# Scan of a selective state-space layer: the product of delta and input is started by a ScalarE copy into PSUM

## The chip, the cores and the metric

The kernel runs on one core of a Trainium2 chip. The metric is the device time of one execution in microseconds (us); lower is better. Times in this text are us unless marked ns.

## The reference, cut to what matters

The whole program is a two-layer decoder (a state-space layer, cross attention and experts, then retention, a ternary attention block and experts again). The change touches only the first stage, for 8 sequences of 100 positions with 1024 inner channels and 16 states:

```
x = silu(conv(x_in))                       # [8, 100, 1024], the "convolved columns"
delta = softplus(x @ wd1.T @ wd2.T + b)    # [8, 100, 1024]
step: h = exp(delta * A_n) * h + (delta * x) * B_n      # for n = 0..15
      y = sum over n of h * C_n
y = (y + W_D * x) * silu(skip)
```

Every later stage needs the result of this one, so nothing else of the network runs beside it, except one by-product: while the scan runs, TensorE makes the keys of the following cross attention.

## The kernel before, in words

`mamba_scan` keeps channels on the 128 partitions and 8 x 100 = 800 columns of time. The 1024 channels are 8 tiles, numbered t = 0 to 7; each tile goes through n = 0 to 15. A Python function `turn` holds two tiles (j = 0 and 1). VectorE runs the first turn straight and the other three in a loop on the chip, so j = 0 is tile 0, 2, 4, 6.

VectorE, per tile: wait for `delta_ready`, then L698 forms `dx = delta * x` into PSUM; per n it forms `drive = dx * B_n` (L704, PSUM to PSUM) and runs the scan L707 over `decay` (SBUF) and `drive` into `state`. After the scan of n = 1 (`FINISH`) it multiplies the finished sums of the previous tile by the gate (L689, four 64x400 pieces, `finish`), which frees the two banks of sums `y`. `own` is a wait on VectorE's own counter `chain_s`, raised by one for each L698 and L704, so 17 a tile.

ScalarE, per tile: wait for `delta_ready`, then per n one exponential (L654) into a ring of RA = 3 `decay` buffers, and after it one key copied out of PSUM (L621, `take_key`, four steps behind, so at n = 0 and n = 1 it takes keys 12 and 13 of the tile before). The other work is put between them by n: the scaled x (L657, n = 6), the two gate halves (L626, n = 8 and 12), the next delta's first step (L631) and its curve Abs, Exp, Ln (L640 to L644, n = 10 to 12), the gate's Silu (L671, n = 14). Exp, Ln and Silu change tables (ACT_TABLE_LOAD).

GpSimd, per n: `seen = state * C_n` (L737), for n in `JOIN` it adds two of them (L740); it clips the next delta (L745) and at n = 13 (`ADD_AT`) adds its last part (L749), which raises `delta_ready`. TensorE makes a key per n (L762), adds `seen` into `y` with an identity (L787; at n = 0 only once `finished` says the banks are free), and makes the gate halves (L772, L775) after n = 4 and n = 8, and the next delta's product (L781). SyncE's queue stores keys and, in tile 0 only, spreads the rows B_n and C_n over all partitions (`spread_row(n + 3)`), row n + 3 once key n - 1 has been taken, which ScalarE does in its step n + 3.

`dx` is columns 0 to 799 and `drive` columns 800 to 1599 of PSUM, in banks of 512 columns.

Of the kernel before, what the change touches and what calls it, by code (L numbers as in the profile page):

```python
# [19 lines left out]
ALU = mybir.AluOpType  # L20
# [3 lines left out]
BANK = 512  # L24
NB = 8
L = 100
T = NB * L
# [61 lines left out]
class Core:  # L89
# [6 lines left out]
    def sem(self, name):  # L96
        self.counting.append(self.nc.alloc_semaphore(name))
        return self.counting[-1]
# [202 lines left out]
N_ST = 16  # L301
# [216 lines left out]
def mamba_scan(c, xc, vec, delta, proj, wd2, keys, ctx_loaded, bC, cC, spread, spread_row, negA, wk, wk_loaded, k_dram):  # L518
# [3 lines left out]
    nc, dram = c.nc, c.dram  # L522
    RA, RH, RV, RS = 3, 4, 2, 2
    with ExitStack() as ctx:
        sb = lambda s, shape, dt=F32: ctx.enter_context(nc.sbuf_tensor("ms_" + s, shape, dt))
        sem = lambda s: c.sem("ms_" + s)
        decay, state = sb("decay", [P, RA, NB, L]), sb("state", [P, RH, T])
        flat = c.psum[:, :, :].rearrange("p b n -> p (b n)")
        dx, drive = flat[:, 0:T], flat[:, T:2 * T]
        y, side_banks = [c.banks[4][:, 0:HALF], c.banks[5][:, 0:HALF]], c.banks[6:6 + RS]  # L530
        positive = sb("positive", [P, T])
        assert 2 * T <= 4 * BANK

        free = c.x_space[:, :, :].rearrange("p b d -> p (b d)")
        part = lambda at, n: free[:, D + at * T:D + (at + n) * T]
        skipw = free[:, 0:D].rearrange("p (k e) -> p k e", k=KD)
        gate, seen = part(0, 1), part(1, RV).rearrange("p (r t) -> p r t", r=RV)
        made = free[:, D + 3 * T:D + 3 * T + 2 * SH].rearrange("p (r s) -> p r s", r=2)
        cleared, decayed, chain_s = sem("cleared"), sem("decayed"), sem("vector_chain")
        skip_loaded, x_scaled = sem("skip_w_loaded"), sem("x_scaled")  # L540
        side_filled, side_taken = sem("side_filled"), sem("side_taken")
# [13 lines left out]
        tile_of = lambda t, i, j: t[:, bass.ds(i * 2 + j, 1), :].rearrange("p a t -> p (a t)")  # L555
        per, TURNS = 2 * N_ST, KE // 2

        FINISH, SCALE, SUM_X, OPEN = 1, 6, 12, 14
        GATE_AT, LAG = [4, 8], 4
        DELTA_AT, CLIP_AT, CURVE_AT, ADD_AT = [1, 2], 5, 10, 13  # L560
        JOIN = [3, 7, 9, 11]
# [54 lines left out]
        @block.scalar  # L616
        def _(act):
            def take_key(t, u, last=False):
                act.wait_ge(side_filled, at_side(t, last, "key", u) + 1)
                act.wait_ge(key_stored[u % 2], t * (8 * N_ST) + 16 * (u // 2) + 16)  # L620
                nc.scalar.copy(made[:, u % 2, :], side("key", u, last)[:, 0:SH]).then_inc(side_taken, 1)  # L621

            def take_gate(t, h, last):
                act.wait_ge(finished, t + 1)
                act.wait_ge(side_filled, at_side(t, last, "gate", h) + 1)
                nc.scalar.copy(gate[:, half(h)], side("gate", h, last)[:, 0:HALF]).then_inc(side_taken, 1)  # L626

            def take_delta(t, j, h):

                act.wait_ge(side_filled, at_side(t, False, "delta", h) + 1)  # L630
                nc.scalar.activation(delta[:, 1 - j, half(h)], side("delta", h)[:, 0:HALF], ACT.Identity,  # L631
                                     bias=vec[:, bass.ds(t + 1, 1), DC + 1:DC + 2].rearrange("p a v -> p (a v)")).then_inc(side_taken, 1)

            def curve(t, j, z):

                act.wait_ge(clipped, t + 1)
                act.wait_ge(curved, t * 3 + z + 1)
                at = delta[:, 1 - j, :]
                if z == 0:
                    ins = nc.scalar.activation(at, at, ACT.Abs)  # L640
                elif z == 1:
                    ins = nc.scalar.activation(at, at, ACT.Exp, scale=-1.0)
                else:
                    ins = nc.scalar.activation(at, at, ACT.Ln, bias=1.0)  # L644
                ins.then_inc(curved, 1)

            def tile(i, j, first=False, last=False):
                t = i * 2 + j
                if not first:
                    act.wait_ge(delta_ready, t)  # L650
                for n in range(N_ST):
                    g = j * N_ST + n
                    act.wait_ge(scanned, i * per + g + 1 + (not first and g < per % RA))
                    nc.scalar.activation(decay[:, g % RA, :, 1:], seqs(delta[:, j, :])[:, :, 1:], ACT.Exp,  # L654
                                         scale=tile_of(negA, i, j)[:, n:n + 1]).then_inc(decayed, 1)
                    if n == SCALE:
                        nc.scalar.activation(tile_of(xc, i, j), tile_of(xc, i, j), ACT.Copy,  # L657
                                             scale=tile_of(vec, i, j)[:, DC + 2:DC + 3]).then_inc(x_scaled, 1)
                    if n >= LAG:
                        take_key(t, n - LAG, last)  # L660
                    elif not first:
                        take_key(t - 1, n - LAG + N_ST)
                    if n - LAG in GATE_AT:
                        take_gate(t, GATE_AT.index(n - LAG), last)
                    if n - LAG in DELTA_AT and not last:
                        take_delta(t, j, DELTA_AT.index(n - LAG))
                    if n - CURVE_AT in range(3) and not last:
                        curve(t, j, n - CURVE_AT)
                    if n == OPEN:
                        act.wait_ge(side_taken, at_side(t, last, "gate", 1) + 1 + RS)  # L670
                        nc.scalar.activation(gate, gate, ACT.Silu).then_inc(gated, 1)  # L671

            act.wait_ge(cleared, 1)
            act.sem_inc(curved, 1)
            tile(0, 0, first=True)
            for t in range(1, KE):
                tile(t // 2, t % 2, last=t == KE - 1)
            for u in range(N_ST - LAG, N_ST):
                take_key(KE - 1, u, True)

        @block.vector
        def _(dve):
            def finish(i, j):

                dve.wait_ge(summed, (i * 2 + j) * SUMS)
                dve.wait_ge(gated, i * 2 + j)
                for r, h in quads:
                    at = placed(r, h)
                    last = nc.vector.tensor_tensor(xc[at, bass.ds(i * 2 + j - 1, 1), half(h)].rearrange("p a t -> p (a t)"),  # L689
                                                   y[r][at, :], gate[at, half(h)], ALU.mult)  # L690
                last.then_inc(finished, 1)

            def turn(i, first):
                own = Chain(dve, chain_s, i, 2 * (1 + N_ST))
                for j in range(2):
                    if not (first and j == 0):
                        dve.wait_ge(delta_ready, i * 2 + j)
                    own(nc.vector.tensor_tensor(dx, delta[:, j, :], tile_of(xc, i, j), ALU.mult))  # L698
                    for n in range(N_ST):
                        g = j * N_ST + n  # L700
                        if first and j == 0:
                            dve.wait_ge(spread[n], 32)
                        dve.wait_ge(scanned, i * per + g + RA)
                        own(nc.vector.tensor_tensor(drive, dx, bC[:, n, :], ALU.mult))  # L704
                        dve.wait_ge(decayed, i * per + g + 1)
                        dve.wait_ge(weighed, i * per + g + 1)
                        nc.vector.tensor_tensor_scan(state[:, n % RH, :],  # L707
                                                     decay[:, g % RA, :, :].rearrange("p b l -> p (b l)"),
                                                     drive, 0.0, ALU.mult, ALU.add).then_inc(scanned, 1)
                        if n == FINISH and not (first and j == 0):  # L710
                            finish(i, j)
                own.close()

            nc.vector.memset(decay[:, :, :, 0:1], 0.0).then_inc(cleared, 1)
            dve.sem_inc(scanned, RA)
            dve.sem_inc(finished, 1)
            turn(0, True)
            with dve.Fori(0, TURNS - 1) as i:
                turn(i + 1, False)
            finish(TURNS, 0)  # L720
# [2421 lines left out]
```

## Time and profile before

| what | value |
|---|---|
| time, median of 3 runs | 2751.64 (2750.43 to 2753.07) |
| the profiled execution | 2748.01, its span 2746.2 |
| TensorE matmul busy | 2451.3 (89%) |
| VectorE busy | 1383.1 (50%) |
| ScalarE busy | 917.4 (33%) |
| GpSimd busy | 658.2 (24%) |
| scan of the state-space layer | from about 89 to 529 of the span |

The table's shares are means over the whole program. The change lies in the stretch from 89 to 529, and the engines there stand otherwise than in the mean. The difference of 1.8 between the profiled execution and its span lies ahead of and behind the span.

### The profile page before, as it was taken

The page shows a single profiled execution, that of the slowest core. Times are in us where ns is not written, and L with a number is a line of the kernel's source. Part 1 is how long each engine was busy: PE and PEld are TensorE (multiplying, and loading weights), DVE is VectorE, ACT ScalarE, POOL GpSimd, SP SyncE. Part 2 cuts the span into 40 slices and gives each one's busy share as a digit, 9 for nine tenths or more (in the row PEclk, how much of TensorE's full clock was granted, in tenths as well). Part 3 has the DMA queues.
Part 4 walks back from the last instruction along what each step waited for, and adds up shares of the span by engine and source line. Part 5 has one row for each costly group of instructions (what it writes and reads, how often), then busy time and mean ns, then how long its engine had stood idle before and what let it go on. Part 6 is the DMA issues. An engine that isn't in the chain of part 4 may idle for free. (4 is left out here: it accounts for less than half of the span.)

```text
span 2746.2 us, 31763 instructions
## 1 busy us (share of the span) xinstructions
PE 2451.3 (89%) x11965; PEld 1238.5 (45%) x11965; DVE 1383.1 (50%) x1941; ACT 917.4 (33%) x1861; POOL 658.2 (24%) x531
## 2 busy tenths in 40 slices
PE   7899999889999999888599799886987579999996
PEld 4344444334555555536345454354664333333332
DVE  5689999521678886731445512386444521111114
ACT  3555565203533334401122110185333112222222
POOL 0477887401000000001201100000000024444433
PEclk9899999999999999998789899998998789999998
DMA  3632222345435444335600100202000162560624
GB/s 106 200 106 87 77 83 92 100 137 206 167 125 178 159 145 115 130 115 205 215 20 0 42 0 3 72 23 92 1 1 1 63 243 94 201 267 26 256 95 140
DMA packets 96587, 301.31 MB, mean 110 GB/s; under 512 B 27018, under 2 KB 57446, under 8 KB 81724
## 3 DMA queue, kind: packets, MB, share of 16 engines
q1 hardware_dynamic: 62784, 171.06, 18.7%
q0 software_dynamic: 33664, 128.35, 12.9%
q8 instruction: 93, 1.52, 0.2%
q14 instruction: 46, 0.38, 0.0%
HBM read 446.13 MB, written 47.22 MB: 180 GB/s over the span
## 5 line engine op out<-in xcount | busy, mean ns | idle before, releaser
L737 POOL TENSOR_TENSOR x_rows<-ms_state,mb_C_everywhere 128x800 f32<-128x800 f32 x128 | 246.7, 1935 | 168.0 <-DVE ms_state L707 135.8
L762 PE MATMUL psum<-mb_context,mb_key_w 128*128 128x361 f32 x768 | 271.4, 492 | 14.7 <-ACT x_rows L621 8.5
L993 PE MATMUL psum<-at_Wv,at_context 128*128 128x512 f32 (+1 forms) x576 | 266.1, 601 | 0.0
L707 DVE TENSOR_TENSOR_SCAN ms_state<-ms_decay,psum 128x800 f32<-128x800 f32 x128 | 233.0, 1820 | 19.1 <-ACT ms_decay L654 14.2
L3008 ACT ACTIVATE tf_hidden<-psum,tf_b 128x64 f32<-128x64 f32 x512 | 111.9, 331 | 364.1 <-PE psum L2964 344.8
L2953 PE MATMUL psum<-tf_W,tf_x_T 128*64 128x512 f32 x1024 | 231.6, 600 | 0.8 <-DVE tf_x_T L3017 0.8
L2975 PE MATMUL psum<-tf_W,tf_hidden 128*64 128x512 f32 x1024 | 226.8, 595 | 0.0
L762 PEld LDWEIGHTS psum<-mb_context,mb_key_w 128*128 128x128 f32 x768 | 141.1, 194 | 147.9 <-issue 44.9
L2888 POOL DMA_INDIRECT tf_W<-in_L_W,tt_weight_row x120 | 119.8, 998 | 183.2 <-PE psum L2953 119.9
L1094 ACT ACTIVATE at_prob<-psum,at_neg_max 100x722 f32<-100x722 f32 x128 | 110.5, 863 | 145.7 <-DVE at_neg_max L1156 145.5
L1156 DVE TENSOR_REDUCE at_neg_max<-psum 100x1 f32<-100x722 f32 x128 | 115.6, 904 | 78.2 <-PE psum L1014 77.8
L654 ACT ACTIVATE ms_decay<-mb_delta,mb_minus_exp_A 128x792 f32<-128x792 f32 x128 | 122.1, 955 | 86.4 <-DVE ms_state L707 72.0
L993 PEld LDWEIGHTS psum<-at_Wv,at_context 128*128 128x128 f32 (+1 forms) x576 | 99.7, 185 | 104.1 <-issue 100.3
L3026 DVE COPY tf_up<-psum 128x512 f32<-128x512 f32 x64 | 44.2, 692 | 202.5 <-PE psum L2953 172.7
L704 DVE TENSOR_TENSOR psum<-psum,mb_B_everywhere 128x800 f32<-128x800 f32 x128 | 127.8, 998 | 18.7 <-DMA mb_C_everywhere<-B_C_dram 13.4
L2953 PEld LDWEIGHTS psum<-tf_W,tf_x_T 128*64 128x64 f32 x1024 | 70.8, 138 | 135.6 <-issue 134.3
L2975 PEld LDWEIGHTS psum<-tf_W,tf_hidden 128*64 128x64 f32 x1024 | 70.4, 137 | 133.5 <-issue 133.5
L2013 PE MATMUL psum<-x_cols,re_w_in 128*128 128x400 f32 (+1 forms) x352 | 120.0, 504 | 1.6 <-ACTq L76 1.6
L3035 DVE TENSOR_TENSOR tf_y<-psum,tf_b 128x512 f32<-128x512 f32 x16 | 11.1, 692 | 214.6 <-PE psum L2975 200.2
L1025 PEld LDWEIGHTS psum<-ident,at_prob 100*128 100x128 f32 x768 | 75.2, 142 | 77.7 <-issue 76.1
L787 PE MATMUL psum<-x_rows,ident 64*64 64x400 f32 x768 | 88.2, 530 | 21.4 <-DVE mb_conv_cols L689 10.1
L1025 PE MATMUL psum<-ident,at_prob 100*128 100x100 f32 x768 | 91.6, 256 | 11.9 <-DVE at_prob_T L1170 11.7
(482 smaller groups left out, 3840.9 us busy)
## 6 DMA issues: line engine op xcount, KB each, us to landing
at_piece<-in_L_W_f POOLq DMA_DIRECT2D x24, 1024.0 KB, 6.5
keys_dram<-x_rows SPq DMA_DIRECT2D x128, 180.5 KB, 1.9
at_k_cols<-keys_dram SPq DMA_DIRECT2D x64, 361.0 KB, 3.2
sf_W<-in_L_W SPq DMA_DIRECT2D x16, 1024.0 KB, 6.7
tf_W<-in_L_W SPq DMA_DIRECT2D x8, 2048.0 KB, 19.6
mb_context<-in_ctxT SPq DMA_DIRECT2D x16, 541.5 KB, 4.6
at_context<-in_ctxT SPq DMA_DIRECT2D x8, 1083.0 KB, 5.0
ternary_dram<-at_piece_made POOLq DMA_DIRECT2D x14, 512.0 KB
```

Of the source, the lines that this page charges most:

```text
L654: nc.scalar.activation(decay[:, g % RA, :, 1:], seqs(delta[:, j, :])[:, :, 1:], ACT.Exp, scale=tile_of(negA, i, j)[:, n:n + 1]).then_inc(d ...
L704: own(nc.vector.tensor_tensor(drive, dx, bC[:, n, :], ALU.mult))
L707: nc.vector.tensor_tensor_scan(state[:, n % RH, :], decay[:, g % RA, :, :].rearrange("p b l -> p (b l)"), drive, 0.0, ALU.mult, ALU.add).t ...
L737: nc.gpsimd.tensor_tensor(seen[:, n % RV, :], state[:, n % RH, :], cC[:, n, :], ALU.mult).then_inc(weighed, 1)
L762: last = nc.tensor.matmul(side("key", u, t == KE - 1)[:, 0:SH], lhsT=wk[:, k, e * P:(e + 1) * P], rhs=keys[:, h, k, :], start=(k == 0), st ...
L993: last = nc.tensor.matmul(bank[0:rows_of(t), :], lhsT=ctxT[:, b % 2, k, t * P:t * P + rows_of(t)], rhs=wv[:, k, h * BANK:(h + 1) * BANK], ...
L1025: last = nc.tensor.transpose(turn_bank(t), prob[:, g % RP, t * P:(t + 1) * P], c.ident[0:L, 0:L])
L1156: nc.vector.tensor_reduce(neg_max[:, g % RP:g % RP + 1], scores(g % 2), mybir.AxisListType.XY, ALU.max, negate=True).then_inc(maxed, 1)
L2013: last = nc.tensor.matmul(ring.bank(n)[0:width(e), 0:HALF], lhsT=w_in[:, k, at + e * P:at + e * P + width(e)], rhs=c.xT[:, k, half(h)], st ...
L2888: nc.gpsimd.indirect_dma_start(dst, None, src, bass.IndirectOffsetOnAxis(ap=fetch[:, z, p:p + 1], axis=0), bounds_check=NE * P - 1, oob_is ...
L2953: ins = nc.tensor.matmul(up[t % 2][cols(z), :], lhsT=xT[p % 2][:, k, cols(z)], rhs=w1[z][:, n, k, :], start=(k == 0), stop=(k == KD - 1))
L2975: ins = nc.tensor.matmul(down[p % 2][cols(z), :], lhsT=hid[:, m, cols(z)], rhs=w2[z][:, m, :], start=(m == 0), stop=(m == KM - 1))
```

## The change

ScalarE copies the tile's convolved columns into `dx` in PSUM; VectorE then multiplies that place by delta, in place, instead of reading both factors from SBUF. In ScalarE's order the copy stands at n = `PLACE` = 2, ahead of that step's exponential, so behind two exponentials and, from tile 1 on, two key copies. It waits until VectorE has formed the last `drive` of the tile before (`chain_s` at 17 per tile), since `dx` is in use until then. VectorE waits for a new semaphore `x_placed` ahead of the multiply. `drive` moves from column 800 to column 1024, so that each of the two has two banks of its own.

```diff
-        dx, drive = flat[:, 0:T], flat[:, T:2 * T]
+        dx, drive = flat[:, 0:T], flat[:, 2 * BANK:2 * BANK + T]
-        assert 2 * T <= 4 * BANK
+        assert T <= 2 * BANK
+        x_placed = sem("x_placed")
-        FINISH, SCALE, SUM_X, OPEN = 1, 6, 12, 14
+        PLACE, FINISH, SCALE, SUM_X, OPEN = 2, 1, 6, 12, 14
...
                     g = j * N_ST + n
+                    if n == PLACE:
+                        if not first:
+                            act.wait_ge(chain_s, t * (1 + N_ST))
+                        nc.scalar.copy(dx, tile_of(xc, i, j)).then_inc(x_placed, 1)
                     act.wait_ge(scanned, i * per + g + 1 + (not first and g < per % RA))
...
-                    own(nc.vector.tensor_tensor(dx, delta[:, j, :], tile_of(xc, i, j), ALU.mult))
+                    dve.wait_ge(x_placed, i * 2 + j + 1)
+                    own(nc.vector.tensor_tensor(dx, dx, delta[:, j, :], ALU.mult))
```

## Rows read from the trace of the kernel before

**Rows 1.** Stretch 300:400: length, busy PE, PEld, DVE, ACT, POOL; clock, DMA share, GB/s.
```profile
300.00:400.00 100.00, 94.65 (x436) 43.97 (x436) 95.33 (x71) 59.74 (x85) 80.43 (x42) 1.00 0.27 87
```

**Rows 2.** Waits between 140 and 540: who waited for whom, total, times, longest.
```profile
ACT ms_decay L654 <- POOL mb_delta L749: 14.2, 7, 6.3
PE psum L787 <- DVE mb_conv_cols L689: 10.1, 7, 2.7
```

**Rows 3.** Instructions of L698: duration min/median/max in ns, first and last start.
```profile
L698 DVE TENSOR_TENSOR psum<-mb_delta,mb_conv_cols x8: 975/2510/2568, 89.4 to 466.0; 128x800 f32<-128x800 f32 x8
```

**Rows 4.** Timeline at the border of tiles 3 and 4, VectorE.
```profile
306.06 1.82 DVE L707 TENSOR_TENSOR_SCAN ms_state<-ms_decay,psum 128x800 f32<-128x800 f32 x1 [0.27 <-ACT ms_decay L654]
307.80 2.55 DVE L698 TENSOR_TENSOR psum<-mb_delta,mb_conv_cols 128x800 f32<-128x800 f32 x1
310.48 1.00 DVE L704 TENSOR_TENSOR psum<-psum,mb_B_everywhere 128x800 f32<-128x800 f32 x1
311.67 1.82 DVE L707 TENSOR_TENSOR_SCAN ms_state<-ms_decay,psum 128x800 f32<-128x800 f32 x1 [0.19 <-DVE psum L704]
```

**Rows 5.** Timeline of the same border, GpSimd.
```profile
307.55 1.93 POOL L737 TENSOR_TENSOR x_rows<-ms_state,mb_C_everywhere 128x800 f32<-128x800 f32 x1
```

**Rows 6.** Timeline at the border of tiles 0 and 1.
```profile
147.22 1.91 POOL L737 TENSOR_TENSOR x_rows<-ms_state,mb_C_everywhere 128x800 f32<-128x800 f32 x1
...
149.38 0.45 ACT L621 COPY x_rows<-psum 128x361 f32<-128x361 f32 x1
150.24 0.97 DVE L698 TENSOR_TENSOR psum<-mb_delta,mb_conv_cols 128x800 f32<-128x800 f32 x1
```

**Rows 7.** Timeline at the border of tiles 3 and 4, ScalarE.
```profile
307.65 0.95 ACT L654 ACTIVATE ms_decay<-mb_delta,mb_minus_exp_A 128x792 f32<-128x792 f32 x1 [1.33 <-POOL mb_delta L749]
...
310.05 0.96 ACT L654 ACTIVATE ms_decay<-mb_delta,mb_minus_exp_A 128x792 f32<-128x792 f32 x1
```

**Rows 8.** ScalarE groups from 140 to 540, shapes apart: busy, mean ns.
```profile
L631 ACT ACTIVATE mb_delta<-psum,mb_vectors 128x400 f32<-128x400 f32 x12 | 7.1, 594 | 4.3 <-PE psum L781 4.3
L657 ACT ACTIVATE mb_conv_cols<-mb_conv_cols,mb_vectors 128x800 f32<-128x800 f32 x7 | 6.6, 947 | 0.0
L644 ACT ACTIVATE mb_delta<-mb_delta 128x800 f32<-128x800 f32 x6 | 5.2, 870 | 0.1
```

**Rows 9.** Timeline at the border of tiles 2 and 3.
```profile
254.80 0.96 ACT L654 ACTIVATE ms_decay<-mb_delta,mb_minus_exp_A 128x792 f32<-128x792 f32 x1 [1.28 <-POOL mb_delta L749]
...
257.48 0.46 ACT L621 COPY x_rows<-psum 128x361 f32<-128x361 f32 x1 [0.52 <-DMA keys_dram<-x_rows]
...
257.98 1.00 DVE L704 TENSOR_TENSOR psum<-psum,mb_B_everywhere 128x800 f32<-128x800 f32 x1 [0.47 <-DVE psum L698]
```

**Rows 10.** Timeline at the border of tiles 4 and 5.
```profile
360.47 0.96 ACT L654 ACTIVATE ms_decay<-mb_delta,mb_minus_exp_A 128x792 f32<-128x792 f32 x1 [1.34 <-POOL mb_delta L749]
...
363.41 1.00 DVE L704 TENSOR_TENSOR psum<-psum,mb_B_everywhere 128x800 f32<-128x800 f32 x1 [0.23 <-DVE psum L698]
```

**Rows 11.** Timeline at the start of tile 0, and its first wait for a spread row.
```profile
90.43 1.00 DVE L704 TENSOR_TENSOR psum<-psum,mb_B_everywhere 128x800 f32<-128x800 f32 x1
90.70 2.65 ACT L654 ACTIVATE ms_decay<-mb_delta,mb_minus_exp_A 128x792 f32<-128x792 f32 x3
91.75 1.82 DVE L707 TENSOR_TENSOR_SCAN ms_state<-ms_decay,psum 128x800 f32<-128x800 f32 x1 [0.33 <-ACT ms_decay L654]
...
103.96 1.00 DVE L704 TENSOR_TENSOR psum<-psum,mb_B_everywhere 128x800 f32<-128x800 f32 x1 [1.51 <-DMA mb_C_everywhere<-B_C_dram]
```

**Rows 12.** Timeline of tile 4: TensorE from the freed sums to the second gate half, and what follows it.
```profile
318.71 0.90 PE L787 MATMUL psum<-x_rows,ident 64*64 64x400 f32 x8 [1.33 <-DVE mb_conv_cols L689]
...
347.83 0.49 ACT L626 COPY x_rows<-psum 128x400 f32<-128x400 f32 x1 [2.44 <-PE psum L772]
...
352.87 1.82 DVE L707 TENSOR_TENSOR_SCAN ms_state<-ms_decay,psum 128x800 f32<-128x800 f32 x1 [1.54 <-ACT ms_decay L654]
```

## The prediction

> **What bounds the kernel now.** The page's chain of waits was read first and gives nothing here: it follows the work that ended last through the experts of the end and doesn't reach back to the scan. That the scan counts in full comes from the code: everything after it needs its output, so each us gained or lost between 89 and 529 is one at the end. So I took the busy time by stretch for that part [rows 1]: between 300 and 400 VectorE is busy for 95.3 of 100, TensorE for 94.7, GpSimd for 80.4, ScalarE for 59.7. A reader should draw two things from it. VectorE and TensorE are both nearly full, so neither alone is plainly the bound, and ScalarE, which gets the new work, is free for 40 of 100. The tempting conclusion is that work moved to ScalarE costs nothing.
>
> The list of who waited for whom says where to doubt that [rows 2]: seven times, once a tile, ScalarE's exponential waited for GpSimd's last part of delta (14.2 in all), and seven times TensorE waited for VectorE's `finish` (10.1). Both lie at the border between two tiles, which is where the change is. So the rest is read from the timeline of the borders.
>
> The round of one tile is this. `finish` frees the sums, and TensorE, which waited 1.33 for it, starts at 318.71. It then works with few gaps to the second gate half, which ScalarE had waited 2.44 for when it copied it at 347.83. Behind that copy stand ScalarE's Ln, two table loads and an exponential, and for that exponential VectorE stood still for 1.54, until 352.87 [rows 12]. Three scans later comes the border, L698, two drives, two scans and the next `finish`. This is a closed round through TensorE, ScalarE and VectorE; a delay anywhere between border and `finish` is handed on to TensorE and comes back at the next border. VectorE's gap of 1.54 doesn't soak it up, since the gate half for which it waits is late by the same amount.
>
> **VectorE's side of the change.** L698 took 2510 ns in the median and 975 at least [rows 3]. At the border of tiles 3 and 4 it began at 307.80 and took 2.55 [rows 4], and a GpSimd multiply ran from 307.55 to 309.48 [rows 5]; the 0.9 left after 309.48 is about the length of the bare operation. At the border of tiles 0 and 1 GpSimd's multiply was over at 149.13, and L698, begun at 150.24, took 0.97 [rows 6]. So six of eight pay about 1.5 for sharing something with GpSimd. The new multiply reads one factor from PSUM and one from SBUF, as L704 does, and L704 took 1.00 beside the same GpSimd work [rows 4]. I take 1.00 and 0.03 to the next start. The gain on VectorE alone is 6 x 1.5 = 9.1.
>
> The Trainium skill (SBUF — State Buffer, section "Who interferes with whom") says the same in a rule: a VectorE instruction with two SBUF inputs contends with a GpSimd instruction that reads SBUF, and one with at most one SBUF input outside the two-port modes doesn't. By that rule too the multiply costs 1.0 and the sum stays; a reader who stops there would forecast 9 us gained.
>
> **ScalarE's side, tile 4.** ScalarE gets `delta_ready` and starts its first exponential of the tile at 307.65; its third starts at 310.05 [rows 7]. The copy is put exactly ahead of that third one, behind two exponentials and two key copies, so it starts at 310.05, 2.40 after the first. Its length is not in the trace: 800 columns from SBUF to SBUF took 0.95 (L657) or 0.87 (L644), and 400 columns with bias out of PSUM 0.59, so 1.19 for 800 [rows 8]. I take L657's 0.95, a copy of the same columns; 0.87 and 1.19 are the bounds. From ScalarE's end to VectorE's start I allow 0.09 (VectorE's scan started at 352.87, its exponential ended at 352.78 by the same timeline). So the multiply starts at 307.65 + 2.40 + 0.95 + 0.09 = 311.09 and the first drive at 312.12, against 310.48 before [rows 4]: 1.64 later. The operation got 1.5 cheaper and yet ends later, as it now waits 3.3 for a copy that stands behind a late `delta_ready`. Queued behind the waiting multiply on VectorE are both drives and scans and `finish`; behind `finish`, TensorE.
>
> The Trainium skill (ScalarE: Activation LUTs, section "Step-by-step: what each stage is for") says that ScalarE reaches PSUM faster than SBUF. It gives no figure; by it the copy would lie near the low bound, 0.08 a tile less than by my row. No row here shows a ScalarE write to PSUM.
>
> **All borders.** Tiles 2 and 6 repeat tile 4 (first exponential to first drive 2.81 and 2.82, against 2.83): 3 x 1.64 = 4.9. Tile 5: first exponential 360.47, drive 363.41 [rows 10], so 2.94 before against 2.40 + 0.95 + 0.09 + 1.03 = 4.47 now: 1.53, and tile 7 has the same: 3.1. At tile 3 the second key copy waited 0.52 for an earlier key's store [rows 9], so the copy can start only at 257.82, and the drive comes at 259.89 instead of 257.98: 1.9. Tile 1: the second key copy starts at 149.38 [rows 6] and holds ScalarE for 0.34, the copy follows at 149.72, the multiply at 150.76 instead of 150.24: 0.5. Tile 0: the three first exponentials from 90.70 take 2.65 [rows 11], 0.86 from start to start, so the copy starts at 92.42, the multiply at 93.46, the drive at 94.49 and the scan at 95.52 instead of 91.75: 3.8. In tile 0 VectorE waits ten times for spread rows, first at 103.96 [rows 11]. Those loads are issued only once ScalarE has taken an old key, which hangs on the scans; they shift with them and I let them absorb nothing.
>
> Sum: 4.9 + 3.1 + 1.9 + 0.5 + 3.8 = 14.2. Against it: in tiles 2, 4 and 6 VectorE stood 0.19 between drive and scan twice, with no late producer in sight [rows 4]. If this is the sequencer catching up after the loop's jump, it will do so during the new wait, at a gain of 3 x 0.38 = 1.1. I take half, 0.55. The banks: `drive` and `dx` no longer meet in one bank, but L704 at 1.00 is 0.02 above L698's least, which leaves nothing worth a term. The wait for `chain_s` is over when the copy comes up (the last drive ends a whole scan before the border). ScalarE's later work shifts by 0.9 into its idle time. Result 13.7 slower. On the profiled execution's 2748.0 that is 2761.7; on the median of the runs shown, 3.6 higher, 2765.3.
>
> **The rivals.** (a) Gaps absorb it: `finish` isn't on the round, TensorE makes up for a later start, and VectorE's standing 1.54 before a late exponential [rows 12] shrinks by what came later. For: TensorE is at 94.7, not full [rows 1]. Against: each tile it waits for `finish` with nothing else to do [rows 2]. Then tiles 2 to 7 cost nearly nothing, tiles 0 and 1 4.3: 2756 (2753 to 2759). Chance 0.13.
>
> (b) The other sign: the copy is hidden. Place: the six later borders. If `delta_ready` came early enough that ScalarE's two exponentials, two keys and copy were done when VectorE ends the tile's last scan, only the cheaper multiply would be left: -9.1 + 4.3 = -4.8, and VectorE's gaps after the loop's jump could take it to -6: 2746. It needs `delta_ready` 3.2 sooner against VectorE (307.88 against 311.09); from 1.6 sooner on, a border neither gains nor loses. Against: ScalarE had just waited 1.33 for GpSimd [rows 7], which works without a pause into that point. Chance 0.07.
>
> (c) The first forecast with the copy at its upper bound and tile 3's store wait at other borders too: 8 x 0.24 + 5 x 0.5 = 4.4 more, 2770. Chance 0.08.
>
> The forecast has 0.72; its own range is 2760 to 2769 (copy at 0.87 and all the small gaps gone: 12.5, tile 0 partly absorbed by its loads: 3 less; copy at 1.1: 1.2 more; the runs spread by 1.5). The whole range, to leave out no more than 2 in 10, takes in part of (a) and nearly (c): 2757 to 2769.5. The measurement can't tell 0.2%, 5.5, from no change, so 2746.1 to 2757.1 counts as same. (a) falls mostly there and (b) half. Slower 0.83, same 0.12, faster 0.05.
>
> **What the profile after would show.** The multiply at 1.00 at all borders, GpSimd's multiply beside it no longer stretched. A wait of about 3.2 ahead of it in tiles 2 to 7, put down to ScalarE's copy, which starts 2.40 after the tile's first exponential and takes 0.95. TensorE's wait for `finish` larger by 1.6 a tile, its other waits as before, and tiles of 54.4 from border to border instead of 52.8 (307.65 to 360.47 [rows 7, 10]). Tile 0's first scan 3.8 later. The prediction is wrong if the tiles stay at 52.8 although the multiply waits (a), or if the multiply doesn't wait (b).

## The result, and the profile after

The changed kernel takes 2770.57 us in the median (2765.96 to 2773.23, 6 runs) against 2751.03 (2742.92 to 2759.05, 6 runs) for the kernel before: a ratio of 1.0076, 95% interval 1.006 to 1.0092. It is slower, as forecast, but by 19.5 us instead of 13.7, and the median lies 1.1 above the upper end of the range.

The profiled execution has a span of 2764.2, 18.0 more than before. VectorE's last `finish` ended at 529.27 before and ends at 547.33 now, 18.06 later, so the whole difference lies ahead of the end of the scan. In the profile after, the copy is L657, the multiply L704, the drive L710, the scan L713, ScalarE's exponential L659, `finish` L694, TensorE's sum L793 and key L768.

The new multiply and the new copy, all eight of each (duration min/median/max in ns, first and last start):

```profile
L704 DVE TENSOR_TENSOR psum<-psum,mb_delta x8: 999/1000/1000, 93.7 to 485.9; 128x800 f32<-128x800 f32 x8
```

```profile
L657 ACT COPY psum<-mb_conv_cols x8: 815/838/842, 92.8 to 485.0; 128x800 f32<-128x800 f32 x8
```

The multiply costs 1.00 everywhere, where L698 had 2.51 in the median [rows 3]. The copy takes 0.84, less than the 0.95 taken from [rows 8]. Of those rows L657, at 0.95, scales each partition by a value of its own; L644, at 0.87, has no such scale, and neither has the copy, so 0.87 was the nearer row. (The Trainium skill, ScalarE: Activation LUTs, section "Step-by-step: what each stage is for", calls PSUM the faster destination for ScalarE. This case agrees faintly: the copy is 0.03 under the shortest SBUF row of the same size, and that row is another function.)

The border of tiles 3 and 4, first ScalarE, then VectorE, then GpSimd, from the timeline:

```profile
317.58 0.96 ACT L659 ACTIVATE ms_decay<-mb_delta,mb_minus_exp_A 128x792 f32<-128x792 f32 x1 [1.30 <-POOL mb_delta L755]
...
319.64 0.45 ACT L622 COPY x_rows<-psum 128x361 f32<-128x361 f32 x1
319.98 0.84 ACT L657 COPY psum<-mb_conv_cols 128x800 f32<-128x800 f32 x1
...
320.85 1.00 DVE L704 TENSOR_TENSOR psum<-psum,mb_delta 128x800 f32<-128x800 f32 x1 [3.00 <-ACT psum L657]
321.99 1.00 DVE L710 TENSOR_TENSOR psum<-psum,mb_B_everywhere 128x800 f32<-128x800 f32 x1
323.18 1.82 DVE L713 TENSOR_TENSOR_SCAN ms_state<-ms_decay,psum 128x800 f32<-128x800 f32 x1 [0.19 <-DVE psum L710]
...
319.80 1.91 POOL L743 TENSOR_TENSOR x_rows<-ms_state,mb_C_everywhere 128x800 f32<-128x800 f32 x1 [0.41 <-PE psum L793]
```

This is the border of [rows 4, 5, 7] again, and it goes as forecast: the copy starts 2.40 behind the first exponential, with the second exponential and two key copies ahead of it, VectorE waits 3.00 for it, and the first drive comes 4.41 after the exponential instead of 2.83. The gap of 0.19 between drive and scan is still there.

What was not forecast shows further on in the timeline. These are TensorE's first sums of tiles 1 to 7, each of which waits for `finish`:

```profile
162.84 0.90 PE L793 MATMUL psum<-x_rows,ident 64*64 64x400 f32 x8 [1.54 <-DVE mb_conv_cols L694]
217.21 0.90 PE L793 MATMUL psum<-x_rows,ident 64*64 64x400 f32 x8 [2.86 <-DVE mb_conv_cols L694]
273.41 1.61 PE L793 MATMUL psum<-x_rows,ident 64*64 64x400 f32 x8 [3.49 <-DVE mb_conv_cols L694]
330.21 1.11 PE L793 MATMUL psum<-x_rows,ident 64*64 64x400 f32 x8 [2.87 <-DVE mb_conv_cols L694]
385.55 1.61 PE L793 MATMUL psum<-x_rows,ident 64*64 64x400 f32 x8 [2.66 <-DVE mb_conv_cols L694]
440.92 0.90 PE L793 MATMUL psum<-x_rows,ident 64*64 64x400 f32 x8 [2.85 <-DVE mb_conv_cols L694]
495.06 1.61 PE L793 MATMUL psum<-x_rows,ident 64*64 64x400 f32 x8 [2.65 <-DVE mb_conv_cols L694]
```

The wait was 1.33 at tile 4 [rows 12]. The sum's own length, 0.90 before in tiles 2 to 7, is 1.11 or 1.61 in four of them: the same matmuls on a slower clock. At tile 2 the sum still took 0.90, and the key behind it took 3.78 instead of 2.09. The busy time by stretch for tiles 2 to 6, cut at the borders (length, busy PE, PEld, DVE, ACT, POOL, granted clock, DMA share, GB/s), shows which tiles were hit:

```profile
204.58:260.17 55.59, 51.64 (x229) 23.90 (x229) 48.13 (x38) 32.68 (x47) 41.99 (x23) 0.97 0.24 78
260.17:317.58 57.41, 52.84 (x229) 24.11 (x229) 48.09 (x38) 32.70 (x47) 42.00 (x23) 0.94 0.24 76
317.58:373.13 55.55, 51.59 (x229) 23.94 (x229) 48.12 (x38) 32.68 (x47) 41.98 (x23) 0.97 0.24 79
373.13:428.28 55.15, 51.45 (x229) 23.71 (x229) 48.07 (x38) 32.70 (x46) 41.89 (x23) 0.97 0.24 79
428.28:482.65 54.37, 49.97 (x230) 23.18 (x229) 48.14 (x38) 32.91 (x47) 42.00 (x23) 1.00 0.25 80
```

Tile 6, where the clock stayed at 1.00, is 54.37 long, the 54.4 of the forecast. The four others are 0.8 to 3.0 longer (at tile 3 about 0.5 of it is a longer wait for a store). The clock term reaches VectorE where the round said a late TensorE would arrive: at its wait for the exponential behind the second gate half, 1.54 before [rows 12]. In tiles 2, 3 and 6:

```profile
252.59 1.82 DVE L713 TENSOR_TENSOR_SCAN ms_state<-ms_decay,psum 128x800 f32<-128x800 f32 x1 [2.76 <-ACT ms_decay L659]
...
310.01 1.82 DVE L713 TENSOR_TENSOR_SCAN ms_state<-ms_decay,psum 128x800 f32<-128x800 f32 x1 [3.99 <-ACT ms_decay L659]
...
475.07 1.82 DVE L713 TENSOR_TENSOR_SCAN ms_state<-ms_decay,psum 128x800 f32<-128x800 f32 x1 [1.54 <-ACT ms_decay L659]
```

Over tiles 2 to 5 this wait grew by 1.22, 2.45, 1.19 and 1.04, 5.9 together.

And it could have been seen beforehand. The kernel before has one wait for `finish` of that size, at tile 1, and TensorE's timeline shows what came after it:

```profile
159.16 1.08 PE L787 MATMUL psum<-x_rows,ident 64*64 64x400 f32 x8 [2.70 <-DVE mb_conv_cols L689]
160.17 3.56 PE L762 MATMUL psum<-mb_context,mb_key_w 128*128 128x361 f32 x6
```

The key took 3.56, where the steady tiles need 2.09, and the granted clock between 161 and 165 was 0.73 on the mean, so for about half of that stretch it was at the lower of its two levels, 1.2 instead of 2.4 GHz. VectorE's wait behind the gate half in that tile was 2.70 instead of 1.54.

### The profile page after: what moved, and what is told of

Its sections match the earlier page's. It is cut to its first block and busy times, and to the rows that moved or that the text cites. A ratio compares the mean times of both kernels' runs of the same rounds, so it can differ in the third digit from the quotient of the medians.

```text
span 2764.2 us, 31772 instructions
## 1 busy us (share of the span) xinstructions
PE 2459.6 (89%) x11965; PEld 1239.6 (45%) x11965; DVE 1375.3 (50%) x1941; ACT 921.4 (33%) x1869; POOL 655.0 (24%) x531
## 5 line engine op out<-in xcount | busy, mean ns | idle before, releaser
L768 PE MATMUL psum<-mb_context,mb_key_w 128*128 128x361 f32 x768 | 275.6, 498 | 14.9 <-ACT x_rows L622 8.6
L713 DVE TENSOR_TENSOR_SCAN ms_state<-ms_decay,psum 128x800 f32<-128x800 f32 x128 | 233.0, 1820 | 23.2 <-ACT ms_decay L659 18.3
L768 PEld LDWEIGHTS psum<-mb_context,mb_key_w 128*128 128x128 f32 x768 | 142.9, 197 | 151.7 <-issue 46.6
L659 ACT ACTIVATE ms_decay<-mb_delta,mb_minus_exp_A 128x792 f32<-128x792 f32 x128 | 122.2, 956 | 90.8 <-DVE ms_state L713 76.0
L710 DVE TENSOR_TENSOR psum<-psum,mb_B_everywhere 128x800 f32<-128x800 f32 x128 | 127.8, 998 | 17.4 <-DMA mb_C_everywhere<-B_C_dram 12.1
L793 PE MATMUL psum<-x_rows,ident 64*64 64x400 f32 x768 | 91.3, 547 | 31.4 <-DVE mb_conv_cols L694 18.9
## 6 DMA issues: line engine op xcount, KB each, us to landing
tf_W<-in_L_W SPq DMA_DIRECT2D x8, 2048.0 KB, 19.5
```

The lines of the kernel that those rows point to most:

```text
L713: nc.vector.tensor_tensor_scan(state[:, n % RH, :], decay[:, g % RA, :, :].rearrange("p b l -> p (b l)"), drive, 0.0, ALU.mult, ALU.add).t ...
L768: last = nc.tensor.matmul(side("key", u, t == KE - 1)[:, 0:SH], lhsT=wk[:, k, e * P:(e + 1) * P], rhs=keys[:, h, k, :], start=(k == 0), st ...
```

## The experiments

Each was compared with runs of the kernel before on its own chip, where that had a median of 2747.0 (21 runs, experiments 1 to 4) or 2745.0 (24 runs, experiments 5 to 8). A ratio is given with its 95% interval; it isn't exactly that of the medians, from which it differs by up to 0.0007. Tile lengths, waits and clocks are from one profiled execution of each.

**1. TensorE's wait filled with work** (on the changed kernel)

```diff
-                for k in range(KC):
+                for k in (*range(KC), *range(KC)) if u == 0 and t else range(KC):
```

> The changed kernel, with the first key of tiles 1 to 7 computed twice by TensorE (three 128x361 products over all 384 context features more, the second pass starts the sums anew, so nothing changes in the result). It puts about 2.0 us of work into TensorE's wait of 2.9 to 3.5 us for finish, in front of it. Theory A (the changed kernel's tiles 2 to 5 are longer than forecast because TensorE's granted clock falls behind that wait, shown at 0.57 to 0.70 in a 4 us stretch): the clock stays at 1.00 in tiles 2 to 6, each is 54.4 us from border to border instead of 55.2 to 57.4, and the kernel is about 6 us faster than the changed one in spite of more work (0.2% to 0.3% under it, ratio to before about 1.0050). Rival B (the extra length comes from the ScalarE copy itself or from the banks): the tiles stay at 55.2 to 57.4 and the ratio at 1.0076 or above.

Measured: 2763.53, ratio 1.0063 (1.0041 to 1.0085). The clock was 1.00 in tiles 2 to 6, four of the five were 54.1 to 54.4 long and one 55.35, where the second key copy waited 0.88 for a store. The trace speaks for theory A, but the interval overlaps the changed kernel's, and that one had run on another chip. Hence experiments 5 and 6.

**2. VectorE delayed by 2.07 a tile, no copy** (on the kernel before)

```diff
                     own(nc.vector.tensor_tensor(dx, delta[:, j, :], tile_of(xc, i, j), ALU.mult))
+                    for _ in range(2):
+                        own(nc.vector.tensor_tensor(drive, dx, delta[:, j, :], ALU.mult))
```

(and the count of `own` per turn raised by 4)

> The kernel before, with two more drive-sized VectorE multiplies behind L698 in every tile (their output is overwritten). No ScalarE copy, no other bank. 2 x 1.03 = 2.07 us of delay a tile between border and finish. Theory A (a closed round through TensorE, and the clock): tiles 1 to 7 get longer by at least 2.07, together with tile 0 +16.5 us, and TensorE's wait for finish of 3.4 brings its clock down, so tiles of 55.5 to 57.5 us and some 6 to 12 us more, +22 to +28 us in all (ratio 1.008 to 1.010). Theory without the clock: +16.5 us (1.0060). Rival (gaps absorb it): VectorE's standing 1.54 and 0.26 us per tile shrink, the tiles stay near 53 and the kernel within 5 us.

Measured: 2777.83, ratio 1.0115 (1.0098 to 1.0132), some 31 us more, above all three. Not all of that is the scan. In the profiled execution the scan stage, from VectorE's first multiply to its last `finish`, took 461.6 instead of 439.9, so 21.7 more, at the lower end of theory A. What comes behind the scan took 2226, against 2217 in the kernel before and 2213 to 2220 in the other runs here; the edit doesn't touch it, and why it was longer stays open.

Tiles 2 to 6 are 57.1, 55.7, 57.0, 55.7 and 57.0 long at clocks of 0.94 and 0.97 in turn; in tiles 2 to 7 every wait for `finish`, 3.03 to 3.35 long, was followed by a sum of 1.50 to 1.61 instead of 0.90. From first exponential to first drive tile 2 lost 2.07, and VectorE's wait behind its second gate half grew by 2.25, from 1.54 to 3.79; the two make up the 4.3 by which it is longer than the 52.75 of before. So in these tiles a delay between border and `finish` costs its full length and the clock on top, without the ScalarE copy, the multiply out of PSUM or the other banks having a part in it. Rival (a) of the prediction, that gaps absorb it, is refuted.

**3. The copy ahead of the wait for `delta_ready`** (on the changed kernel, L657 taken out of the steps)

```diff
                 if not first:
+                    act.wait_ge(chain_s, t * (1 + N_ST))
+                    nc.scalar.copy(dx, tile_of(xc, i, j)).then_inc(x_placed, 1)
                     act.wait_ge(delta_ready, t)
...
+            nc.scalar.copy(dx, tile_of(xc, 0, 0)).then_inc(x_placed, 1)
             act.wait_ge(cleared, 1)
```

> The changed kernel with the copy taken out of the steps and put ahead of ScalarE's wait for delta_ready (it needs the convolved columns and a free place, not delta), in tile 0 ahead of the wait for the cleared decay columns. ScalarE stands idle there for 1.3 us and the copy takes 0.81. Theory A (placement is everything): VectorE never waits for the copy in tiles 1 to 7, the multiply takes 1.00, the first drive comes 1.56 sooner than in the kernel before; TensorE's wait of 1.33 for finish shrinks to nothing and bounds the gain, so 6 x 1.3 = 8 us gained, 0.7 lost in tile 0: about 2744 us, ratio 0.9973, clock 1.00 in tiles 2 to 7. Rival B (ScalarE writing PSUM, or the multiply from PSUM, costs something by itself): ratio at or above 1.000.

Measured: 2741.27, ratio 0.9986 (0.9973 to 0.9999). Tiles 2 to 6 take 51.9 to 52.0, clock 1.00. VectorE waits for the copy only in tile 0 (0.70). Rival B falls, by the tiles more than by the ratio, whose interval ends just under 1: with the same copy and the same multiply, put elsewhere, tiles 2 to 7 are each shorter than before. But the gain is smaller than expected, 0.7 to 0.95 a tile (0.8 on the mean of tiles 2 to 6) instead of 1.3, and the ratio shows half of it. VectorE's timeline says why:

```profile
311.79 2.23 DVE L693 TENSOR_TENSOR mb_conv_cols<-psum,x_rows 64x400 f32 x4 [0.60 <-PE psum L792]
...
314.07 0.90 PE L792 MATMUL psum<-x_rows,ident 64*64 64x400 f32 x8 [0.46 <-DVE mb_conv_cols L693]
```

`finish` (here L693) now waits 0.60 for TensorE's last sum of the tile before, and TensorE in turn still waits 0.46 for `finish`, since the key that it makes meanwhile (2.09) starts 0.27 ahead of the four multiplies (2.23) and is shorter. Each of the two now waits for the other, so TensorE's work and `finish` set the pace of this version, and a still earlier multiply would only lengthen the wait of 0.60.

**4. The move of `drive` alone** (on the kernel before)

```diff
-        dx, drive = flat[:, 0:T], flat[:, T:2 * T]
+        dx, drive = flat[:, 0:T], flat[:, 2 * BANK:2 * BANK + T]
```

> The kernel before with drive moved to column 1024 and nothing else. Both theories: no difference, within 0.1%, L704 at 1.00 and L698 at 2.5 us. Were the two banks the cause of the extra 6 us, it would be 0.2% slower.

Measured: 2746.39, ratio 1.0001 (0.9988 to 1.0015). L704 took 1.00 and L698 2.5, and tiles 2 to 6 were 52.6 to 52.8 long. So the banks are not the cause of the extra 6 us; an effect under about 0.15% isn't excluded by the times.

**5. The changed kernel again, beside 6**

> The changed kernel once more, on the same chip as the next one, since the first comparison of the two went over two chips and their intervals overlapped. Ratio to before 1.006 to 1.009; in the trace the clock falls behind TensorE's wait for finish in several of tiles 2 to 7, and each tile so hit is 1.0 to 2.5 us longer than 54.4.

Measured: 2768.65, ratio 1.0084 (1.0068 to 1.0101). Tiles 1 to 6 are 55.2, 56.9, 58.0, 55.5, 55.3 and 54.4 long; all but the last of them have a clock under 1.00.

**6. The filled wait again**

> The changed kernel with the first key of tiles 1 to 7 computed twice, once more. Clock theory: 4 to 6 us faster than the changed kernel on the same chip, so a ratio to before 0.0015 to 0.002 lower, tiles 2 to 6 at 54.3 and clock 1.00. If only the trace of one execution had it: no difference between the two ratios.

Measured: 2757.47, ratio 1.0047 (1.0032 to 1.0061), 11.2 below experiment 5 on the same chip, with intervals apart. That is twice what was expected, since in experiment 5 the clock's fall cost more than in the first trace of the changed kernel: VectorE's wait behind the gate half was 2.72, 4.06, 4.10, 2.70 and 2.67 in tiles 1 to 5, together 8.6 over 1.54 each. With the wait filled it was 1.54 or 1.55 in all of them. In the two traces the scans end 10.4 apart, so this wait is most of it. Tile 3 in the stretch view, against the 57.41 above:

```profile
258.76:313.15 54.39, 51.75 (x235) 24.27 (x235) 48.09 (x38) 32.97 (x47) 41.97 (x23) 1.00 0.25 80
```

TensorE does three products more (six records of 235) and the tile is shorter. The clock was 1.00 in tiles 1 to 7. This shows the clock as the cause of the extra time.

**7. PLACE = 0** (on the changed kernel)

```diff
-        PLACE, FINISH, SCALE, SUM_X, OPEN = 2, 1, 6, 12, 14
+        PLACE, FINISH, SCALE, SUM_X, OPEN = 0, 1, 6, 12, 14
```

> The changed kernel with PLACE = 0: the copy stands behind delta_ready but ahead of the first exponential. The multiply then starts 0.9 us after delta_ready instead of 3.3, the first drive 0.8 to 0.9 sooner than in the kernel before. Theory (the round counts what lies between delta_ready and finish): 0.85 a tile gained against the kernel before in tiles 2 to 7, so 51.9 to 52.0 us a tile, TensorE's wait for finish about 0.5, clock 1.00, 0.8 lost in tile 0: ratio 0.998 to 0.999. Rival (the copy's place matters only as a wait of VectorE that other gaps absorb): as the changed kernel, 1.007.

Measured: 2742.90, ratio 0.9993 (0.9977 to 1.0009), tiles 2 to 6 at 52.1, clock 1.00, TensorE's wait 0.44 to 0.46. The kernel as a whole can't be told from the one before; its tiles are 0.5 to 0.8 shorter. Two exponentials and two key copies ahead of the copy are the difference between this and 1.0084.

**8. VectorE delayed by 1.03 a tile** (on the kernel before; experiment 2 with `range(1)`)

> The kernel before with one more drive-sized VectorE multiply (1.03 us) behind L698 in every tile, half of the earlier delay. Round without the clock: 8 x 1.03 = 8.2 us, tiles of 53.8, ratio 1.0030. TensorE then waits 2.1 to 2.4 us for finish, less than the 2.65 to 3.5 behind which the clock was seen to fall. Clock theory with a dependence on the wait: clock 1.00 in most of tiles 2 to 6 and so 1.0030, far less than half of what the double delay cost (1.0115). If the clock falls here too, up to 1.0055.

Measured: 2757.18, ratio 1.0042 (1.0027 to 1.0058), 12.1 us more, between the two expectations. My supposed order, that the clock falls only behind waits over 2.6, was wrong. TensorE waited 1.98 to 2.32 in tiles 2 to 7. The clock stayed at 1.00 in the stretch of tile 2, behind 2.32, and fell to 0.97 in those of tiles 3 to 6, behind 1.98 to 2.31; those tiles are 54.6 to 55.0 long instead of 53.8. Tile 2, with the delay and no fall of the clock, was 53.79 long against 52.75 before: a delay of 1.03 cost 1.04. At tile 6:

```profile
431.87 1.61 PE L789 MATMUL psum<-x_rows,ident 64*64 64x400 f32 x8 [2.31 <-DVE mb_conv_cols L689]
433.41 2.98 PE L764 MATMUL psum<-mb_context,mb_key_w 128*128 128x361 f32 x6
```

## Why the prediction was wrong

The direction and the round held, and one term was missing.

**VectorE's side.** The multiply at 1.00 at every border: right, and GpSimd doesn't slow it, also not in experiment 3, where at tile 4 it ran from 304.02 to 304.99, wholly beside a GpSimd multiply from 303.76 to 305.67, and took 0.97. GpSimd's second multiply of the tile, which took 2.22 to 2.29 while it started beside the end of L698, fell back to 1.91, as forecast.

**The borders.** From the tile's first exponential to the first drive, tiles 2 to 7 lost 1.59, 2.15, 1.58, 1.56, 1.59 and 1.56, together 10.0, where 9.9 was forecast, and tile 1 0.44 for 0.5. That is partly luck, as two errors of 0.1 nearly cancelled: the copy was shorter and VectorE's next instruction came 0.1 later behind the multiply. The term of 0.55 for the 0.19 gaps was wrong: they stayed, and what causes them isn't shown.

**Tile 0.** The first scan came 4.0 later, 0.4 of it from before the scan stage, but by the next border only 2.8 were left for the 3.8 forecast. VectorE's ten waits for spread rows shrank from 13.4 to 12.1 in total, so they do absorb about 1.

**The round.** "A delay anywhere between border and `finish` is handed on to TensorE and comes back at the next border": experiments 2 and 8 show it for a delay, experiments 3 and 7 for an earlier multiply, and tile 6 at 54.37 gives the forecast number. "VectorE's gap of 1.54 doesn't soak it up": right.

**The step that failed** is "TensorE's wait for `finish` larger by 1.6 a tile, its other waits as before, and tiles of 54.4". The wait did grow by 1.6 a tile (2.2 at tile 3). What I left at zero, without giving a reason, is what TensorE does behind it: with 2.65 to 3.49 of idling the granted clock fell in most tiles, and the next key and sums ran slower, so that VectorE's wait behind the gate half grew by 5.9 over tiles 2 to 5. Tile 1, which had this drop already, lost it in this execution, for a gain of 1.1: there the clock fell sooner, behind a wait of 2.27 for a key copy (key 2.67 from 151.91, sum 1.61), and the wait for `finish` was only 1.54. That was luck, as experiment 5 has a wait of 3.14 there and VectorE's 2.72. In the balance of the profile, start 0.4, tile 0 2.8, borders 10.5, the wait behind the gate half 5.9 - 1.1 and the last tile's end -0.3 make 18.2, against 18.06 measured. Experiments 5 and 6 put the clock's share on one chip at 11.2 of 23.6 us. What is left with the wait filled is 12.4 us by the medians, near the forecast of 13.7; in experiment 1, with four runs, it was 16.5.

The Trainium skill (TensorE: Matmul & The Clock Gate, section "HAM oscillation — how this bites in real kernels") describes this case in kind: a repeated wait, there for a DMA, that lets the clock fall each round, so that the transition is paid each time. Here the wait is for VectorE, and the clock fell in most rounds, not in all: in five of tiles 2 to 7, not in tile 6. I read the clock at 1.00 in [rows 1] and took it for a constant.

**The rivals.** (a) is refuted by experiment 2. (b), the hidden copy, is what experiment 3 builds: it needs no sooner `delta_ready`, only a copy that doesn't stand behind it. Its price of -4.8 (2747) compares with -3.8 by the ratio of 0.9986 and -5.7 by the medians. (c) gave 2770, the time measured, by another mechanism that didn't occur: the copy took 0.84 and not 1.19, and the wait for a store stayed at tile 3 (its border lost 2.15, the others 1.6).

Open is why the clock stayed at 1.00 behind one wait and fell behind another. It stayed behind 2.32 at tile 2 of experiment 8 and behind 2.86 at tile 6 of experiment 5; it fell behind 1.98 at tile 3 of experiment 8, and behind the same 2.86 at tile 2 of the changed kernel. The traces show the outcome, not the cause.

## What to carry to other kernels

An engine with 40% of its time free is free on average, not at the instant at which its result is wanted: look at which wait and which queued instructions stand ahead of the moved work, and put it ahead of the wait if its inputs allow. When a change lengthens a regular wait of TensorE, look in the trace of before for a wait of the new length and read the lengths of the matmuls after it; there you see whether the clock can fall and what it costs. And the engine that sheds work gains only up to the next one in the round, here TensorE: in experiment 3 the first drive came about 1.55 sooner behind the first exponential, and a tile gained 0.8.

## What was not expected of the hardware

TensorE's granted clock falls behind waits as short as 1.98 in stretches in which it is over 90% busy on the whole, and in tiles 2 to 6 such a fall cost 1.0 to 2.6 us by the growth of VectorE's wait (eight 64x400 matmuls 1.61 instead of 0.90, a key up to 3.98 instead of 2.09). It isn't a plain function of the wait: 2.86 and 2.32 passed without a fall. Giving TensorE 2.0 us of useless matmuls in that wait made the kernel 11.2 us faster than without them.
